# A Mamba-and-gated-MLP block: the down projection's low-rank product is added to its weights on the chip, and the first pass prepares only the up blocks

## The reference

```python
mod = (silu(c) @ wmod).reshape(1, 6, 1, -1)
sa, ca, ga, sb, cb, gb = (mod[:, i] for i in range(6))      # ga, gb kept away from zero
h = layernorm(x) * (1 + ca) + sa
x = x + ga * ssm(h)            # softplus(dt), exp(dt*A), scan over the tokens, D*h
h = layernorm(x) * (1 + cb) + sb
# matmul_lora(x, w, a, b) = x @ w.T + (x @ a.T) @ b.T
gate = matmul_lora(h, gate_w, gate_a, gate_b)
up = matmul_lora(h, up_w, up_a, up_b)
hidden = silu(gate) * up
x = x + gb * matmul_lora(hidden, down_w, down_a, down_b)
```

## Time and profile before

| | |
|---|---|
| median of 3 runs | 2283.12 us (2280.43 to 2285.51) |
| profiled execution, its own time | 2287.54 us |
| its span, first to last instruction | 2285.8 us |
| TensorE, share of the span busy | 89% |
| GpSimd, VectorE, ScalarE | 68%, 63%, 46% |
| mean granted TensorE clock | 0.95 of full speed |
| moved by the DMA queues | 603 MB, 264 GB/s |

### The profile page before, as it was taken

The page is one execution under the profiler, slowest core; times in us unless marked ns, Lnnn a source line. Parts: engine busy times, 40 slices in busy tenths (PEclk is TensorE's granted clock), DMA queues, the critical chain, the costliest instruction groups (busy, mean ns, idle before and its releaser), DMA issues.

```text
span 2285.8 us, 33007 instructions
## 1 busy us (share of the span) xinstructions
PE 2040.8 (89%) x11652; PEld 1855.5 (81%) x11652; DVE 1444.3 (63%) x2119; ACT 1046.5 (46%) x2330; POOL 1543.1 (68%) x960
## 2 busy tenths in 40 slices
PE   7586766888879989899999899999899999999999
PEld 3233235777878989789999799999799999999999
DVE  5665776868767778776778666778667774211111
ACT  3776865656554555444554354555344332210000
POOL 1577879998988877877876877877769895110100
PEclk9788867989989999999999999999999999999999
DMA  9799976778977677576667576767577877787786
GB/s 342 295 367 335 306 281 225 284 262 270 325 259 282 236 256 277 208 263 236 236 229 278 186 259 236 244 228 275 186 263 248 285 253 260 254 290 270 256 289 218
DMA packets 121203, 602.98 MB, mean 264 GB/s; under 512 B 10576, under 2 KB 23120, under 8 KB 80464
## 3 DMA queue, kind: packets, MB, share of 16 engines
q1 hardware_dynamic: 121040, 600.89, 74.5%
HBM read 514.63 MB, written 86.21 MB: 263 GB/s over the span
## 4 chain that ended last, share of the span: by engine, by line
PE 56%; DVE 13%; POOL 9%; issue 8%; ACT 8%; DMA 6%; DVEq 0%; ACTq 0%; SPq 0%; POOLq 0%
PE FP L780 48%; DVE ring L1184 6%; POOL ring L1298 4%; PE FP L663 4%; DVE ring L1069 2%; DMA wts<-w_scratch 2%; POOL y L1273 2%; DMA raw<-w_gu 2%; DVE FP L1159 2%; ACT SC L851 1%; PE FP L804 1%; POOL wts L1281 1%; ACT sqb L969 1%; PE FP L741 1%; POOL xlo L1289 1%
## 5 line engine op out<-in xcount | busy, mean ns | idle before, releaser
L780 PE MATMUL FP<-xhi,wts 128*128 128x368 f32 (+2 forms) x4320 | 1074.2, 325 | 66.6 <-ACT dtb L974 29.4
L780 PEld LDWEIGHTS FP<-xhi,wts 128*128 128x128 f32 x4320 | 770.4, 193 | 77.3 <-issue 60.2
L1298 POOL TENSOR_TENSOR ring<-ring,c_row 128x736 f32<-128x736 f32 (+2 forms) x336 | 575.2, 1712 | 252.8 <-ACT hst L868 252.3
L851 ACT ACTIVATE SC<-dtb,aneg 128x368 f32<-128x368 f32 (+2 forms) x768 | 411.8, 545 | 715.4 <-DVE ring L1184 714.3
L780 PE MATMUL FP<-xlo,wts 128*128 128x368 f32 (+2 forms) x2160 | 697.9, 323 | 0.0
L780 PE MATMUL FP<-hhi,wts 128*128 128x368 f32 (+5 forms) x2376 | 573.4, 322 | 31.9 <-POOL hlo L1313 24.6
L1184 DVE TENSOR_TENSOR_SCAN ring<-SC,hst,ring 128x368 f32<-128x368 f32 (+1 forms) x640 | 579.8, 948 | 3.4 <-ACT SC L851 3.4
L1273 POOL TENSOR_TENSOR y<-y,ring 128x736 f32<-128x736 f32 (+1 forms) x320 | 554.9, 1734 | 13.9
L780 PEld LDWEIGHTS FP<-hhi,wts 128*128 128x128 f32 (+1 forms) x2376 | 408.9, 186 | 39.1 <-POOL hlo L1313 23.6
L780 PEld LDWEIGHTS FP<-xlo,wts 128*128 128x128 f32 x2160 | 416.7, 193 | 1.1
L780 PE MATMUL FP<-hlo,wts 128*128 128x368 f32 (+5 forms) x1188 | 380.5, 320 | 0.0
(11 more groups left out here) (104 smaller groups left out, 1938.2 us busy)
## 6 DMA issues: line engine op xcount, KB each, us to landing
wts<-w_scratch SPq DMA_DIRECT2D x249, 1152.0 KB, 5.2
wts<-w_scratch SPq DMA_DIRECT2D x91, 896.0 KB, 4.9
wts<-w_scratch SPq DMA_DIRECT2D x51, 1024.0 KB, 5.4
w_scratch<-wts SPq DMA_DIRECT2D x44, 1152.0 KB, 8.8
raw<-w_gu SPq DMA_DIRECT2D x44, 576.0 KB, 6.6
modw<-mod_w SPq DMA_DIRECT2D x24, 1024.0 KB, 11.0
w_scratch<-wts SPq DMA_DIRECT2D x16, 896.0 KB, 6.7
w_scratch<-wts SPq DMA_DIRECT2D x9, 1024.0 KB, 7.6
```

The costliest lines, as they stand in the source:

```text
L780: last = mm(out, w, x, start=(start and k == 0 and e == 0), stop=(stop and k == n - 1 and e == 2))
L851: A(decays(c, n, a), tile_of(dtb, c, i), ACT.Exp, scale=aneg[:, i * NS + s:i * NS + s + 1]).then_inc(a_da[a], 1)
L1298: G.tensor_tensor(buf, buf, over_pair(c_of(k)), ALU.mult).then_inc(g_hc, 1)
```

## The change

The low-rank product of the down projection is added to `down_w` on the chip, once, in `FIRST`. The 24 blocks of down weights are now all prepared there. A transfer brings `down_b` beside each, and one transfer `down_a` for all, into a buffer of the modulation matrix. For a block with 7 (8) hidden blocks TensorE makes 7 (8) fp32 matmuls of 128 columns with 16 rows (`mrg`, in two halves), and VectorE adds each half to the raw weights (`madd`), ahead of the split. `FIRST` has 47 `prep` pieces: `lora_a`, 22 gate and 24 down blocks. They go through three buffers instead of two, the third being another buffer of the modulation matrix, which from its block 10 on has three buffers instead of five.

The units `lora_down`, `tda`'s part in them and the two small instructions behind them are gone: a pass has 69 units. The first pass prepares the 22 `up` units and nothing else; for these, `pieces_at` counts 14 matmuls less room for pieces two units ahead of them. The first two `down` units of part 2 are run as one: all but the last hidden block of both, then the last of both; the pieces of the second stand ahead of the first.

```diff
-    UNITS += [("lora_down", part, 0)] + [("down", part, m) for m in range(ND)]
+    UNITS += [("down", part, m) for m in range(ND)]
...
-OTF = [u for u in range(NU) if u % 3 == 1]
-PREP = [u for u in range(NU) if u not in OTF]
+OTF = [u for u in range(NU) if UNITS[u][0] == "up"]
+PREP_RAW = [0, 1, 0, 1] + [(2, 0, 1)[i % 3] for i in range(NPREP - 4)]
...
         while done < NPREP and done - PREP_BEFORE < (NPREP - PREP_BEFORE) * (n + 1) / last:
+            if not wholes or len(downs) * len(WHOLES) >= len(wholes) * len(DOWNS) and banks_open(out) < BANKS - 1:
+                order.append(downs.pop(0))
+                out += [("mrg", done, 0), ("madd", done, 0), ("mrg", done, 1), ("madd", done, 1)]
+            else:
+                order.append(wholes.pop(0))
             out.append(("prep", done))
...
+def room(c, u):
+    return passes(u) - (LOW_PASSES if c == 0 and u + AHEAD_LO in OTF else 0)
...
+    at[LAST_DOWN] += at[LAST_DOWN + 1]
+    at[LAST_DOWN + 1] = []
...
+            def merge(i, h):
+                if h == 0:
+                    pe.wait_ge(d_ad, 16)
+                    pe.wait_ge(d_prep[PREP_RAW[i]], 16 * raw_nth(i))
+                bank_free(pe, "mrg", i, h)
+                for k in halves(PREP[i])[h]:
+                    last = mm(FP[:, BANK["mrg", i, h], to:to + P], down_a[:, at:at + P], down_b, start=True, stop=True)
+                last.then_inc(pe_mrg, 1)
...
+                elif kind == "madd":
+                    dve.wait_ge(pe_mrg, 2 * MERGED.index(i) + h + 1)
+                    V.tensor_tensor(prep_raw(i)[:, at], FP[:, BANK["mrg", i, h], 0:len(ks) * P], prep_raw(i)[:, at], ALU.add).then_inc(v_mrg, 1)
...
             def prep_hi(i):
-                act.wait_ge(d_prep[i % RAW_SLOTS], 16 * (i // RAW_SLOTS + 1))
+                if i in MERGED:
+                    act.wait_ge(v_mrg, 2 * MERGED.index(i) + 2)
...
+                    if step == "begin":
                         pe.wait_ge(g_hlo, c * NH + k1 - 1)
+                        products(out, pairs[:-1], stop=False)
+                        return
+                    if step == "end":
                         pe.wait_ge(g_hlo, c * NH + k1)
+                        last = products(out, pairs[-1:], start=False)
+                    else:
+                        pe.wait_ge(g_hlo, c * NH + k1)
+                        last = products(out, pairs)
...
+                    if u == LAST_DOWN:
+                        unit(c, u, "begin")
+                        unit(c, u + 1, "begin")
+                        unit(c, u, "end")
+                        unit(c, u + 1, "end")
```

More of the change, by code:

```diff
@@ L206, in period_pieces, with raw_before, raw_nth, raw_next @@
     return [(p, w or weight(p)) for p, w in out]
-OTF = [u for u in range(NU) if u % 3 == 1]
-PREP = [u for u in range(NU) if u not in OTF]
-NPREP = len(PREP)
+OTF = [u for u in range(NU) if UNITS[u][0] == "up"]
 PREP_BEFORE = 4
+WHOLES = [u for u in range(NU) if UNITS[u][0] in ("lora_a", "gate")]
+DOWNS = [u for u in range(NU) if UNITS[u][0] == "down"]
+NPREP = len(WHOLES) + len(DOWNS)
+PREP_RAW = [0, 1, 0, 1] + [(2, 0, 1)[i % 3] for i in range(NPREP - 4)]
+def raw_before(i):
+    return ([None] + [x for x in range(i) if PREP_RAW[x] == PREP_RAW[i]])[-1]
+def raw_nth(i):
+    return len([x for x in range(i + 1) if PREP_RAW[x] == PREP_RAW[i]])
+def raw_next(i):
+    return next((x for x in range(i + 1, NPREP) if PREP_RAW[x] == PREP_RAW[i]), None)
+def halves(u):
+    n = PARTS[UNITS[u][1]][1] - PARTS[UNITS[u][1]][0]
+    return [range(0, 4), range(4, n)]
+def bank_freed(item):
+    kind = item[0]
+    if kind in ("sum", "sq"):
+        return ("cen" if kind == "sum" else "norm", *item[1:], PAIRS - 1)
+    return {"proj": ("xs", *item[1:]), "dt": ("keep", *item[1:]), "row": ("rowc", *item[1:]), "mrg": ("madd", *item[1:]),
+            "col": ("late", late_of(item[1]) if kind == "col" else None)}[kind]
+def banks_open(pieces):
+    held = [p for p in pieces if p[0] in ("sum", "sq", "proj", "dt", "row") or p[0] == "col" and p[1] == LATES[late_of(p[1])][0]]
+    return len([p for p in held if bank_freed(p) not in pieces])
 def first_pieces():
@@ L265, in first_pieces @@
         out += tail(0, n)
-    return out
-FIRST = first_pieces()
+    return out, order
+FIRST, PREP = first_pieces()
+MERGED = [i for i in range(NPREP) if PREP[i] in DOWNS]
 SCAN_SHARE = 0.985
+LAST_DOWN = unit_at("down", len(PARTS) - 1, 0)
+LOW_PASSES = 14
+def room(c, u):
+    return passes(u) - (LOW_PASSES if c == 0 and u + AHEAD_LO in OTF else 0)
 def pieces_at(c):
     pieces = period_pieces(c)
-    total, full = sum(w for _, w in pieces), sum(passes(u) for u in range(NU))
-    at, done, u, ended = [[] for _ in range(NU)], 0.0, 0, passes(0)
+    total, full = sum(w for _, w in pieces), sum(room(c, u) for u in range(NU))
+    at, done, u, ended = [[] for _ in range(NU)], 0.0, 0, room(c, 0)
     for piece, w in pieces:
@@ L279, in pieces_at @@
             u += 1
-            ended += passes(u)
+            ended += room(c, u)
         if piece[0] is not None:
@@ L302, in free_at @@
             return place.get(("unit", *divmod(g, NU)), len(order))
[L303 to L305 removed]
+        return place[bank_freed(item)]
     bank, before, last = {}, {}, [None] * BANKS
     for i, item in enumerate(order):
[L309 removed]
+        if item[0] not in ("unit", "sum", "sq", "proj", "dt", "row", "mrg", "col"):
             continue
@@ L707, in piece @@
                     mod_cols(p[1])
+                elif kind == "mrg":
+                    merge(p[1], p[2])
                 elif kind == "sum":
@@ L1043, in _ @@
                         before(*divmod(g - 1, NU))
-                    if u and last == "lora_down":
-                        after(c, u - 1)
                     for p in PIECES[c][u]:
```

170 lines of the change are left out of this document (96 added, 74 removed).

## The result

The changed kernel takes 2318.71 us (median of four runs, 2317.83 to 2323.89) beside 2281.77 us for the one before on the same chip: a ratio of 1.0154 (1.0136 to 1.0173), 37 us slower where 61 us faster was forecast. The profiled execution has a span of 2322.1 us (2285.8 before) and a mean granted clock of 0.929 (0.950).

A forecast was written before the change was run, and what follows sets the result against it. It took TensorE to bound the last two passes and mostly the third and fourth, GpSimd the first, no engine the first scan. 2287.5 - 53.6 - 14.0 - 3 + 10 = 2226.9, as median 2222 us; range 2208 to 2240.

The forecast's parts named there:

- The last two passes: Passes five and six, where TensorE is busy without a gap: each loses 66 matmuls at 0.166 us, 11.0 us.
- the 53.6: Last five passes: removed low-rank matmuls save 11.0 us in each of four and 9.6 in the 320-column pass.
- The first scan, +10: Before the passes: 19 us of additions on the path, 9 back from buffers and order; net 10 us longer.
- The bound of 45: First scan, upper bound: 45 us longer with all additions and an extra TensorE-to-VectorE hand-over in each block.
- slower: Rival, first scan: TensorE blocks at each merge for its raw block, adding 91 us, 2303 in all; chance 0.03.
- The first pass, -3: First pass, where GpSimd sets the pace with hardly changed work: 3 us gained, bounds 12 and -8.
- The rival of a low clock: Rival, first pass: TensorE idles more, falls to the low clock, pass 31 us longer, 2257 in all; chance 0.03.
- The wait at the last hidden block, 14.0: Passes two to four: TensorE's wait for `hlo` shrinks, 4.8 us saved in each, taken as 14.0 together.
- the scan sets the pace of passes two to four: Rival, middle passes: GpSimd and VectorE pace them, so 9.6 + 22 + 14 us aren't won, 2268; chance 0.06.
- The clock at that place: Sums behind the `hlo` wait: 5.11 instead of 6.06 us without it; a removed wait returns more than its length.

The follow-up runs named there:

- fifteen_in_pass: Changed kernel without merges, first pass preparing only 15 units, every third of gate and up: 0.9787 of the kernel before, first pass 320.7 us.
- gates_in_pass: Changed kernel without merges, first pass preparing the 22 gate units instead of the up units: 0.9763 of the kernel before, first pass 325.1 us.
- before_ups: Kernel before, only the first pass changed to prepare the 22 up units, with 14 matmuls less room: ratio 1.0069, first pass 334.8 us.
- merge_matmuls_only: Changed kernel with the merge matmuls but without VectorE's additions: 0.9902 of the kernel before, passes beginning at 369.0 us.
- adds_late: Changed kernel with additions one scan group behind their matmuls in 19 of 24 blocks: 1.0038 of the kernel before, passes beginning at 394.8 us.

## Why the prediction was wrong

- **The last two passes** (22 us of the 53.6): right. 66 matmuls at 0.166 us a start gave 11.2 and 11.0 us. Here TensorE has no wait, and work taken away is time taken away.
- **The first scan, +10.** This is the step that failed: "TensorE's part lies in idle time as long as it runs a group ahead of VectorE; ahead of the scan is then only what VectorE does itself." It does not run a group ahead: the broadcasts have two buffers and wait for VectorE's products, so each product stands behind what VectorE has just released, and VectorE's addition behind the product. The prices of the operations were right, as the rows below show: the products are 38.8 + 24.9 = 63.7 us of TensorE, within 42 to 79; an addition takes 0.688 and 0.556 us, where 0.665 and 0.55 stood. But the sum had nothing for the products and 19 us for the additions. Alone they cost 20.5 and 14.5 us, and their coupling, with the lower clock that came with it, 42.4. That is 58.4 us too little; the relief by buffers and order, 9 in the sum, was 19.8, 10.8 more. Together this is the 48 us. The bound of 45 didn't hold, since it counted the additions and one short extra hand-over in each block, and the rows show 38 waits, 2.3 us each in the mean.
- **The rival "slower"** had the right place, TensorE at each merge, and the wrong cause: nowhere from 78 to 390 us does a product wait for its raw block. It was to decide from 2.9 us per merge on, and the merge costs 77.4/24 = 3.2 us. I gave it 0.03 because the loads would be on time, and they are; the wait is for TensorE's turn.
- **The first pass, -3.** Wrong from "GpSimd sets the pace" on: low parts on another engine made it longer, seven fewer brought 4.4 us. The choice of units costs 13.5 us by itself, 9.8 of it (measured without the merge) by preparing the up and not the gate unit of a pair. What the remaining 4 us are is open; crowding is a candidate, since fifteen_in_pass has 4.4 us less than gates_in_pass. The work taken away won nothing here: the first pass of the changed kernel is 335.6 us, that of before_ups, which still has the low-rank units, 334.8. The rival of a low clock puts the cost at 31 us, but its own numbers give 350 - 321 = 29.
- **The wait at the last hidden block, 14.0**: at the place itself the forecast held. In the third pass TensorE reaches the last block 12.3 us after the last `up` unit, as worked out, waits 1.80 us where 1.6 was forecast, and goes on after 14.1 us (13.9 forecast, 18.7 before). What failed is the step from there to the pass: that the rest of the pass keeps its waits. 15.8 us of waits before are 15.9 after: 4.9 for ScalarE's `dtb` in one place instead of 4.0 in three, 2.5 for GpSimd's `y` ahead of the sums, 2.1 of issue. These three stand ahead of the last block, between 1218 and 1348 us. The pass gained 9.0 us, less than the 11.0 of removed work alone: TensorE is busy 316.2 instead of 325.3 us. In the fourth pass it is busy 7.2 us less, its waits grow from 15.4 to 19.3 us, 1.9 of it for a weight load, and the pass gained 3.4. Of the forecast 45.6 us in passes two to four 13.4 came. This fits the rival "the scan sets the pace of passes two to four", to which I gave 0.06: TensorE waits little there, but it waits for the scan's engines, and what is taken from it comes back in part as another wait. In the second pass the joined units are 3 us of what is missing. It looks worse still beside before_ups, which has the same choice of units: there the second pass is 319.0 us, and the changed kernel needs 324.2, though TensorE is busy 5.0 us less. Its waits are 33.1 instead of 22.8 us, 12.4 instead of 7.0 of them for `dtb` and a new 5.1 for GpSimd's `y`. Why these waits come, link by link, I haven't tested.
- **The clock at that place**: the sixteen sum instructions took 5.11 us in the third pass instead of 6.06, as forecast. For the pass the step that a removed wait gives back more than its length was not confirmed, because the removed wait was replaced: the mean granted clock fell from 0.96 to 0.95 in the second pass, from 0.99 to 0.98 in the third and from 0.99 to 0.97 in the fourth.

Groups of instructions, shapes apart, after (busy us, mean ns | idle before, releaser), for the prices of the merge:

```profile
L766 PE MATMUL FP<-raw,modw 16*128 16x128 f32 x220 | 38.8, 331 | 20.0 <-ACT dtb L1097 13.2 <-DVE mod L1237 3.3 <-DVE raw L1243 3.1
...
L766 PE MATMUL FP<-modw 16*128 16x128 f32 x132 | 24.9, 347 | 3.3 <-DVE modw L1243 3.1 <-ACT dtb L1097 0.2
...
L1243 DVE TENSOR_TENSOR raw<-FP,raw 128x512 f32<-128x512 f32 x20 | 13.8, 688 | 42.0 <-PE FP L766 42.0
...
L1243 DVE TENSOR_TENSOR raw<-FP,raw 128x384 f32<-128x384 f32 x10 | 5.6, 556 | 5.5 <-PE FP L766 5.5
```

## What to carry to other kernels

An engine with idle time takes new work for nothing only if it can do it before someone waits; read in the timeline how far ahead of its consumer it really is, and what stands before the new instruction in its queue. A producer and a consumer placed side by side in two in-order queues can cost more than the two works together (77 against 35 us here, the lower clock of that stretch included); a group of other work between them took back 31. And the busiest engine of a stage isn't its pace: ask what its waits are for, and expect the time won on an engine that waits a little to turn into another wait.

## What the runs showed of the hardware

In a stretch of fp32 matmuls of 128 columns over 16 rows, the granted clock was 0.71 and 0.80; with the same matmuls over 128 rows, zeros in the rest, it was 0.90 and 0.83, though TensorE was busy 94 instead of 108 us of 122. Seven such matmuls over 16 rows (fourteen instructions) took 1.82 us at the high level of the clock (granted 1.00 in that stretch) and 3.35 us at the low one (0.50); halves of the 256-column ones in the earlier trace rows give 1.65 and 3.12.

Timeline of TensorE, after, a block's seven products at the low and at the high level:

```profile
89.72 3.35 PE L766 MATMUL FP<-raw,modw 16*128 16x128 f32 x14
...
184.44 1.82 PE L766 MATMUL FP<-raw,modw 16*128 16x128 f32 x14
```

But rows are not the whole of it: with 16 rows and no additions (merge_matmuls_only) the clock was 0.83 and 0.86, and with 16 rows and late additions (adds_late) 0.81 and 0.78, so it changes with what stands between the products too. A subtraction of 1152 fp32 columns in SBUF took GpSimd 2.65 us (2.61 to 2.70 in the first pass) and VectorE 1.74 in the mean (1.35 to 2.52).
